# Sixteen-head attention stages with their opening steps reordered and their scratch blocks laid out anew, and an attention over eight sequences with biases added on TensorE and all its products on VectorE

## The reference

```python
qkv = x @ qkv_w.T + qkv_b                      # layer 3 a; layer 2 a is the same kind
q, k = rope(q, pos), rope(k, pos)
scores = einsum('bhqd,bhkd->bhqk', q, k) / sqrt(8)
scores = where(causal, scores, -inf)
y = softmax(scores) @ v ; return y @ proj_w.T + proj_b
```

```python
qkv = x @ Wqkv + bqkv ; q, k = apply_rotary(q), apply_rotary(k)   # position = sequence
attn = softmax(causal(q k^T / sqrt(8))) ; return (attn @ v) @ Wout + bout
```

## Time and profile before

| | us |
|---|---|
| median of three runs | 4628.32 |
| lowest, highest | 4628.16, 4641.85 |
| the profiled execution's own time | 4627.72 |
| its span, first to last instruction | 4626.0 |
| TensorE busy in it | 3021.5 (65%) |
| VectorE busy | 2815.2 (61%) |
| GpSimd busy | 2095.7 (45%) |
| ScalarE busy | 1710.7 (37%) |
| mean of the granted TensorE clock | 0.799 |

### The profile page before, as it was taken

How to read it: one execution, slowest core, us unless ns; L and a number is a source line. 1 busy time by engine, 2 the same in 40 slices (tenths; PEclk the granted TensorE clock), 3 DMA queues, 4 the chain that set the end, 5 groups by cost and what they waited for, 6 DMA issues and landing times. The chain is left out here.

```text
span 4626.0 us, 67869 instructions
## 1 busy us (share of the span) xinstructions
PE 3021.5 (65%) x23727; PEld 1870.4 (40%) x23727; DVE 2815.2 (61%) x5972; ACT 1710.7 (37%) x3042; POOL 2095.7 (45%) x2616
## 2 busy tenths in 40 slices
PE   5758267765294549667677745677565787566856
PEld 3658011111294238456233334333243333244534
DVE  4634476674445963432676578577586766496768
ACT  2413156564131224433355412455422445323511
POOL 6552320100343532232345376254594444496676
PEclk9879578897597769878699867799776899676867
DMA  5022222220131012011222000322001222000000
GB/s 153 38 76 69 64 77 67 58 52 1 60 95 47 0 53 63 14 39 53 69 72 64 22 1 0 84 65 76 2 1 28 71 70 57 1 0 1 1 0 19
DMA packets 218177, 206.37 MB, mean 45 GB/s; under 512 B 50439, under 2 KB 195015, under 8 KB 217080
## 3 DMA queue, kind: packets, MB, share of 16 engines
q1 hardware_dynamic: 205560, 176.85, 13.8%
q0 software_dynamic: 12288, 25.19, 1.8%
HBM read 103.55 MB, written 96.47 MB: 43 GB/s over the span
## 5 line engine op out<-in xcount | busy, mean ns | idle before, releaser
L923 DVE TENSOR_REDUCE l0b_negm<-l0b_ps_s 128x2 f32<-128x1024 f32 x256 | 304.5, 1220 | 146.6 <-PE l0b_ps_s L699 145.8
L787 ACT ACTIVATE l0b_E<-l0b_ps_t 128x1024 f32<-128x1024 f32 x256 | 262.0, 1023 | 201.5 <-PE l0b_ps_t L681 201.1
L923 DVE TENSOR_REDUCE l3a_negm<-l3a_ps_s 128x2 f32<-128x256 f32 (+3 forms) x256 | 198.9, 818 | 93.8 <-PE l3a_ps_s L705 93.4
L923 DVE TENSOR_REDUCE l2b_negm<-l2b_ps_s 128x2 f32<-128x256 f32 (+3 forms) x256 | 199.0, 818 | 88.2 <-PE l2b_ps_s L705 87.6
L923 DVE TENSOR_REDUCE l2a_negm<-l2a_ps_s 128x2 f32<-128x256 f32 (+3 forms) x256 | 198.8, 818 | 87.0 <-PE l2a_ps_s L705 86.7
L787 ACT ACTIVATE l3a_E<-l3a_ps_t 128x768 f32<-128x768 f32 (+1 forms) x192 | 169.2, 881 | 186.9 <-PE l3a_ps_t L681 186.7
L787 ACT ACTIVATE l2a_E<-l2a_ps_t 128x768 f32<-128x768 f32 (+1 forms) x192 | 169.4, 882 | 184.2 <-PE l2a_ps_t L681 183.9
L787 ACT ACTIVATE l2b_E<-l2b_ps_t 128x768 f32<-128x768 f32 (+1 forms) x192 | 169.4, 882 | 151.2 <-PE l2b_ps_t L681 151.1
L867 POOL TENSOR_SCALAR_AFFINE_SELECT l3a_E<-l3a_E 128x256 f32<-128x256 f32 x256 | 101.4, 409 | 221.1 <-ACT l3a_E L787 218.9
L867 POOL TENSOR_SCALAR_AFFINE_SELECT l2a_E<-l2a_E 128x256 f32<-128x256 f32 x256 | 101.4, 409 | 219.2 <-ACT l2a_E L787 216.9
L867 POOL TENSOR_SCALAR_AFFINE_SELECT l2b_E<-l2b_E 128x256 f32<-128x256 f32 x256 | 101.3, 410 | 219.1 <-ACT l2b_E L787 218.9
(11 more groups left out here) (1003 smaller groups left out, 9501.2 us busy)
## 6 DMA issues: line engine op xcount, KB each, us to landing
l0b_stack<-l0b_q_piece SPq DMA_DIRECT2D x48, 128.0 KB
l0b_stack<-l0b_k_piece SPq DMA_DIRECT2D x48, 128.0 KB
room_up<-l0b_stack SPq DMA_DIRECT2D x32, 192.0 KB, 3.4
room_down<-l0b_stack SPq DMA_DIRECT2D x32, 192.0 KB, 4.3
l2a_stack<-l2a_q_piece SPq DMA_DIRECT2D x48, 128.0 KB
l2a_stack<-l2a_k_piece SPq DMA_DIRECT2D x48, 128.0 KB
room_up<-l2a_stack SPq DMA_DIRECT2D x32, 192.0 KB, 4.1
room_down<-l2a_stack SPq DMA_DIRECT2D x32, 192.0 KB, 5.0
```

The costliest lines, as they stand in the source:

```text
L787: act.activation(probs(n % 3, c, 0)[:, 2 * p:2 * p + 2, :], ps_t[:, :, 0:width[c]], ACT.Exp, scale=scale).then_inc(probs_ready.sem, 1)
L923: e = dve.tensor_reduce(negm[:, qt, :, j], ps_s[n % 2][:, :, off:off + keys[qt]], AX.X, ALU.max, negate=True)
```

## The change

In the sixteen-head stages the schedule of `normed_at` is replaced by four tables, one for each kind of work of RowNorm; sequences 0 and 1 are both normalised ahead of the clock; q of sequence 0 is cut in one go on GpSimd; the rows of ones are copied at the first step; the scratch has its 48 rows as six blocks of eight outside the heads, and each piece goes out in one DMA with its copies made by a broadcast source (three DMAs for q and three for k, same bytes). In l1a the bias is turned on eight partitions only, cut into three bfloat16 pieces, and added in PSUM by one more matrix product for each sequence; the output bias is a matrix product with one row of ones, for each half; all products are on VectorE; GpSimd keeps only the roots and the bias's pieces. One small weight (rope_rows) is loaded more, and GpSimd makes one more constant (pick_rows) at the start of the program. `normed` is renamed `out_normed` where it meant the normalisation of the output.

```diff
+            pool.memset(core.pick_rows[:, :, :], 0.0).then_inc(made, 1)
+            for k in range(3):
+                r = slice(32 * k, 32 * k + 32)
+                pool.affine_select(out=core.pick_rows[r, :, :], in_=core.pick_rows[r, :, :], compare_op=ALU.not_equal, fill=1.0, base=0,
+                                   pattern=[[-1, B], [0, P]], channel_multiplier=1).then_inc(made, 1)
...
-Q_ROWS = ((0, 8, 24), (16, 40), (32,))
-K_ROWS = ((0, 16, 32), (8, 40), (24,))
+Q_ROWS = (slice(0, 3), slice(4, 6), slice(3, 4))
+K_ROWS = (slice(2, 5), slice(0, 6, 5), slice(1, 2))
...
-        stack = nc.dram_tensor(f"{name}_stack", [2, 4, STACK, 4, S], BF16).ap()
+        stack = nc.dram_tensor(f"{name}_stack", [2, BLOCKS, 4, HD, 4, S], BF16).ap()
...
-        def normed_at(T):
-
-            n = (T + 2 * STEPS - L) // 2 + 1
-            return n if T >= L - 2 * STEPS and T % 2 == 0 and n < B else None
+        def named(table, T):
+
+            return [n for n, at in table.items() if at == T + 2 * STEPS]
+
+        counted = {n: n - 2 for n in range(2, B)} if grouped else {2: 0, 3: 1, 4: 2, 5: 7, 6: 8, 7: 9}
+        rooted = {n: n - 1 for n in range(2, B)} if grouped else {2: 1, 3: 3, 4: 4, 5: 8, 6: 9, 7: 10}
+        shifted = {n: n for n in range(2, B)} if grouped else {2: 1, 3: 7, 4: 8, 5: 9, 6: 10, 7: 11}
+        normed = {n: L + 2 * n for n in range(2, B)} if grouped else {2: 5, 3: 9, 4: 25, 5: 27, 6: 29, 7: 31}
+        split_at = 5 if grouped else 2
...
-                for part, rows in zip(piece[a], (Q_ROWS, K_ROWS)[a]):
-                    for r in rows:
-                        sp.dma_start(stack[a, :, r:r + HD].rearrange("b r c s -> b (r c) s"), part[:, :]).then_inc(pieces_stored[a].sem, 16)
+                for part, places in zip(piece[a], (Q_ROWS, K_ROWS)[a]):
+                    copies = len(range(*places.indices(BLOCKS)))
+                    sp.dma_start(stack[a, places].rearrange("k b d c s -> (b d c) k s"),
+                                 part[:, :].rearrange("p (a s) -> p a s", a=1).broadcast_to([P, copies, S])).then_inc(pieces_stored[a].sem, 16)
...
-                                     stack[a, 2 * hh + half]).then_inc(stack_ready[half].sem, 16)
+                                     stack[a, :, 2 * hh + half].rearrange("k d c s -> k d (c s)")).then_inc(stack_ready[half].sem, 16)
...
-                if T == -L:
+                if T == -2 * STEPS:
                     for u in range(2):
                         for hh in range(2):
                             sp.dma_start(ks[u][64 * hh + M_ROW:64 * hh + M_ROW + 3, :, :], core.ones_rows[:, :]).then_inc(ones_placed.sem, 16)
...
             rows.transposes(pe, 0)
+            rows.transposes(pe, 1)
             for T, b, g, l in steps():
-                if normed_at(T) is not None:
-                    rows.transposes(pe, normed_at(T))
+                for n in named(normed, T):
+                    rows.transposes(pe, n)
...
             for T, b, g, l in steps():
-                if normed_at(T) is not None and normed_at(T) >= 2:
-                    rows.roots(pool, normed_at(T))
+                for n in named(rooted, T):
+                    rows.roots(pool, n)
+                if T == split_at - 2 * STEPS:
+                    for k in range(6):
+                        split(pool, ch, 0, 0, k)
...
-                if normed_at(T) is not None:
-                    rows.shifts(dve, normed_at(T))
-                    if normed_at(T) + 1 < B:
-                        rows.statistics(dve, ch, normed_at(T) + 1)
+                for n in named(shifted, T):
+                    rows.shifts(dve, n)
+                for n in named(counted, T):
+                    rows.statistics(dve, ch, n)
```

and in `batch_attention_stage`:

```diff
-                    pe.matmul(ps_p[b % 2][:, :], xT[i % 2][:, b, :], turned_w[:, b, :], start=True, stop=True).then_inc(proj_in_psum.sem, 1)
+                    pe.matmul(ps_p[b % 2][:, :], xT[i % 2][:, b, :], turned_w[:, b, :], start=True, stop=False)
+                    if i == 0 and b == 0:
+                        pe.wait_ge(bias_ready.sem, bias_ready.upto(1))
+                    pe.matmul(ps_p[b % 2][:, :], core.pick_rows[:, b, :], bias_piece[:, :], start=False, stop=True).then_inc(proj_in_psum.sem, 1)
...
+                    pe.matmul(ps_o[n][:, :, :], core.ones[0:1, :], bo[0:1, :].rearrange("p (a d) -> p a d", a=1).broadcast_to([1, HALF, D]),
+                              start=True, stop=False, skip_group_check=True)
...
             roots(0)
-            turn_bias()
-            roots(1)
-            last_scores(0)
-            add_out_bias(0)
-            add_bias(1)
-            for i in range(TURNS):
-                if i + 2 < TURNS:
-                    roots(i + 2)
-                one_value(i)
-                if i + 1 < TURNS:
-                    last_scores(i + 1)
-                    add_out_bias(i + 1)
-                if i + 2 < TURNS:
-                    add_bias(i + 2)
+            bias_pieces()
+            for i in range(1, TURNS):
+                roots(i)
...
-                for b in range(B - 1):
-                    if i >= 1 and b in (0, HALF):
-                        dve.wait_ge(bias_added.sem, bias_added.upto(2 * (i - 1) + b // HALF + 1))
+                for b in range(B):
+                    if i >= 1:
+                        dve.wait_ge(proj_read.sem, proj_read.upto(B * (i - 1) + b + 1))
                     p = scores_of(dve, i, b)
...
                 for c in range(B):
-                    if c != POOL_K:
-                        values_of(dve, i, c).then_inc(weighted_ready.sem, 1)
+                    values_of(dve, i, c).then_inc(weighted_ready.sem, 1)
```

169 lines of the change are left out of this document (76 added, 93 removed).

## The result

The changed kernel takes 4495.15 us (median of four, 4488.23 to 4499.53); the kernel before took 4631.32 beside it on the same chip (four, 4628.16 to 4641.85). The ratio is 0.970, interval 0.968 to 0.972: 3.0% faster. The profiled execution took 4499.53 us, with a span of 4497.8 us against 4626.0.

What follows compares the result with a forecast made beforehand. Slow stores on 4 of 16 DMA engines were taken to bound the heads, GpSimd to slow VectorE in l1a. Heads 67 + after T = 0 18 + l1a 22 - start 0.5 = 106.5 us: 4521 us, range 4495 to 4577.

Steps and rivals of the forecast that it cites:

- The bound: In l2a's head, no compute engine is the bound for most of it; stores move 96 GB/s at share 0.27, like 4 of 16 engines.
- Rivals A and C: A: stores stay at 96 GB/s, 4577 us, chance 0.10. C: loads left one engine, about 4980 us, chance 0.03.
- Heads, forecast 67: Four heads up to T = 0 get shorter: 15.8 us each in l2a and l3a, 15.5 in l2b, 20 in l0b.
- Each takes 2.05 us plus 0.85 for the reader: Sequence 1's four projections on TensorE before l2a's first score: 2217 + 4 x 2.9 + 1.5 = 2230.3.
- TensorE would be late next: In l2a, sequence 1's four projections, not the load, set the first score: 2230.3 against 2243.1, gain 12.8 us.
- k, not q, is late next: In l2a's head, q is ready at 2210.4 instead of 2217.6, k's cut ends at 2214.0.
- The load, +2 (0 to +4): The stack's load, from six blocks of eight rows on six engines, takes 2 us more than 6.6.
- After T = 0, forecast 18 (0 to 24): With faster stores mT lands 2 to 3 us sooner, shortening TensorE's waits in l2a and l3a: 18 us gained.
- l1a, forecast 22: Stage l1a: preamble 5, turn 0 13.4, turns 1 and 2 4.5 and 5.5, less 6.5: 22 us gained (15 to 27).
- the price of 0.86: In l1a, each us of GpSimd work costs VectorE about 0.86 us; 12 us less in the preamble gives 10.
- Rival B: TensorE sets l1a's turn; only preamble and turn 0 gain, less the tail: 8 us, total 4535, chance 0.13.
- Start, -0.5: At the program's start, rope_rows is one more issue of SyncE on which the first norm waits: 0.5 us lost.

Runs made afterwards that it cites:

- the run with single copies: Changed kernel with its layout of blocks kept, but each copy of a piece stored by its own DMA, twelve for a sequence, no repeated source: ratio 0.972.
- the run with interleaved rows: As the run with single copies, but a block's 48 rows interleaved (channel outside, piece inside), stores 32 slowest in DRAM, loads 48 rows: 4522.84 us, ratio 0.971.

## Why the prediction was right or wrong

The sum was 106.5 us, and the stages gained 128.2: heads 9.7 more than forecast, after T = 0 12.7 more, l1a 2.2 less. The lower end of the range was 4495 us, "heads 75, after T = 0 24, l1a 27, rounded"; these parts give 4502.

**The bound.** Right for the stores. Four engines in the stores, sixteen now: 96 to 262 GB/s, in single microseconds 347, and the run with single copies shows that it is the slowest dimension. The Trainium skill, DMA: Bandwidth & Descriptors, "Why a DMA increments its semaphore by 16 and not by 1", has the number of engines as the largest up to 16 that divides the slowest dimension of both sides; the traces agree in four cases, 4 blocks with a share of 0.27, 6 with at most 0.41, 48 rows with 1.02, 128 with 0.99. Rivals A and C fell with it. But "18.9 us for 1.5 MB of stores, 6.6 for the load" was not all that held the first score of l2a: it has no wait for a DMA, and TensorE's own list, transposes and the projections of sequence 1, ended last in the kernel before.

**Heads, forecast 67, measured 76.7.** In l2a and l3a the step that failed is "Each takes 2.05 us plus 0.85 for the reader": three of the four projections of sequence 1 took 1.12 us, since TensorE was granted the faster clock there (0.97 and 1.00 in the windows). That is 2.8 of the 3.8 us by which l2a's first score came sooner than forecast (36.9 us after the first statistics instead of 40.7); 0.9 is that the projections started sooner, 26.5 instead of 27.4. The kernel before had shown both levels for these projections, 1.12, 1.59 and 2.07 us. It is not a constant of the schedule: in the run with interleaved rows three of them took 2.07 us, and its head is 3 us longer. From the first score to T = 0 l2a gained 3.3 us, the forecast 3, and l3a 5.4; in another execution of the changed kernel l3a took 2.0 more there. mT's path gave the 3 us, but not by the rows of ones, as the sum had it: putting them back costs 1 us in l0b and none in l2a and l2b (57.2 and 58.7).

That TensorE would be late next was right for l2a, l2b and l3a, and the runs show it to be worth more than the text said: with the old table it holds the first score by itself, 19.5 us later. The prediction counted the new table as a condition of one step; undoing it alone costs 48.5 of the heads' 76.7 us, undoing the layout alone 46.4.

l2b came out as forecast (14.9 for 15.5). l0b's 20.0 for 20 is luck: the first score came 14.1 us sooner instead of 12, although it waits 3.19 us for the slower load, and from there to T = 0 it gained 5.9 instead of 8.

"k, not q, is late next" was right (q stored at 20.3 us, k at 23.9). The 7 us given for q were too few: with the new tables, a q cut by steps is 12.5 us late.

**The load, +2 (0 to +4).** 9.3 us from issue to first score instead of 6.6: +2.7, of which l2a's first score waits 0.25, l0b's 3.19. Six engines moved 26 GB/s each, near the upper of the two estimates (24), not 15.

**After T = 0, forecast 18 (0 to 24), measured 30.7.** The step that failed is the upper bound, taken from the wait's rows alone: 11.7 + 12.4. The wait itself was read about rightly, 9.8 us in l2a at equal clocks. The rest of l2a's 18.3 is the granted clock: 0.96 for 0.92 gives 8.5 us more. l3a gained 16.0; by the layout alone it is 15.3, at 0.92 against 0.91. "I take 18, since part returns as waits for ScalarE" is not what happened: TensorE waits as long for ScalarE with and without the layout (21.4 and 20.6 us).

Why l2a had the faster clock stays open. Of thirteen profiles without the old layout ten show 0.95 to 0.97 in this stretch and three 0.92; the three with the old layout and the old order 0.92, 0.92 and 0.94. That looks as if shorter waits brought it. But l0b, over its stretch, had 0.83 to 0.88 without the old layout and 0.86 to 0.87 with it, and no run holds the one and moves the other. l0b's loss of 6.7 is not shown to be the change's: the changed kernel again took 521.9 and 526.3 there.

**l1a, forecast 22, measured 19.8.** Preamble 7.9 instead of 5, turn 0 14.6 instead of 13.4, turns 1 and 2 5.7 + 4.4 instead of 4.5 + 5.5. These rest on the durations of the same products without GpSimd, and these came out within 0.1 us: all scores 5.52 for 5.6, values 5.44 for 5.5. In the preamble VectorE's four turning operations fell by 9.0 us, for which the price of 0.86 gave 10, though GpSimd's bias work fell only to 11.2 us, not 7. The Trainium skill, SBUF — State Buffer, "Who interferes with whom", says that a VectorE instruction with two inputs in SBUF contends with one of GpSimd that reads SBUF; the products, both inputs in SBUF, fell from 15.07 to 4.30 us when GpSimd had none, which agrees. The last turn and the tail cost 12.9 instead of 6.5, and the step that failed is the price of TensorE's products there: the four bias products took 2.07, 2.07, 1.73 and 2.07, 7.9 us for the 6 taken, and the sum left out that the output products around them would run at the lower clock too, 8.3 us instead of 4.8. Rival B did not come about in the turns (VectorE waits 2.2 us in turn 2, for ScalarE), only in the tail.

**Start, -0.5.** 0.16 was measured.

So the mechanisms were right and three sizes failed: the heads of l2a and l3a, the part after T = 0 and the tail of l1a. In the first the lower level of TensorE's clock had been taken throughout, in the second the clock had been left out, in the third it stayed lower than the sum took it.

## What to carry to other kernels

When two chains end at the same time, price the change of each alone: in this kernel two parts gave 30 and 27 us singly and 77 together, and a table of steps that costs nothing was worth as much as a DMA layout. A wait's row bounds what removing it gives only at an unchanged clock: here 9.8 us of 11.7 in l2a, and 18.3 with the clock. Compare stretches with equal granted clock to separate the two. Where a DMA's share stays at a fraction such as 0.27 while its engine waits, look at the slowest dimension of both its sides first. And put small additions such as a bias into the cheap number format before they go onto the engine that ends the stage.
